# Attention scores over groups of 32 rows, two heads in one product, two units issued by turns

## The reference

```python
xs = x[:, global_idx, :]                      # 128 rows of each segment of 256
qh = xs.reshape(b, n_seg, k, NUM_HEADS, HEAD_DIM)
scores = jnp.einsum('bsqhd,bskhd->bshqk', qh, qh) * scale
attn = jax.nn.softmax(scores, axis=-1)
seg_out = jnp.einsum('bshqk,bskhd->bsqhd', attn, qh)
a_os = seg_out.reshape(b, n_seg * k, d)
a_denoms = a_os.sum(axis=-1)                  # the mixing weights come from these sums
```

## Time and profile before

| | |
|---|---|
| median of three runs | 1491.39 us (1488.74 to 1492.62) |
| the profiled execution | 1493.54 us |
| its span | 1491.6 us |
| TensorE busy in the span | 1366.6 us (92%) |
| VectorE busy | 885.0 us (59%) |
| GpSimd busy | 794.1 us (53%) |
| ScalarE busy | 656.6 us (44%) |
| granted TensorE clock, mean of the span | 0.959 |
| attention | from the start to about 139 us |

### The profile page before, as it was taken

How to read it: one execution, slowest core, us unless ns; L and a number is a source line. 1 busy time by engine, 2 the same in 40 slices (tenths; PEclk the granted TensorE clock), 3 DMA queues, 4 the chain that set the end, 5 groups by cost and what they waited for, 6 DMA issues and landing times. The chain is left out here.

```text
span 1491.6 us, 28870 instructions
## 1 busy us (share of the span) xinstructions
PE 1366.6 (92%) x9215; PEld 1202.3 (81%) x9216; DVE 885.0 (59%) x1767; ACT 656.6 (44%) x1170; POOL 794.1 (53%) x696
## 2 busy tenths in 40 slices
PE   8997599999999993899969999999999987999997
PEld 3444488888888883777768999999999977999997
DVE  5788422222222223577568887888888844666655
ACT  4554433233333331666544444543443434555553
POOL 6663197777660003231039887987887855350500
PEclk9997799999999997899979999999999998999999
DMA  4112425222220004210032274475465485465450
GB/s 166 56 33 74 136 79 155 95 98 99 101 96 11 13 15 134 68 57 1 1 113 85 80 205 126 143 195 132 148 187 143 145 286 191 155 214 184 149 201 30
DMA packets 112523, 171.45 MB, mean 115 GB/s; under 512 B 6384, under 2 KB 97648, under 8 KB 106320
## 3 DMA queue, kind: packets, MB, share of 16 engines
q1 hardware_dynamic: 103440, 156.27, 32.7%
q0 software_dynamic: 3408, 9.31, 2.2%
q10 hardware_dynamic: 5616, 5.11, 1.0%
HBM read 115.22 MB, written 55.44 MB: 114 GB/s over the span
## 5 line engine op out<-in xcount | busy, mean ns | idle before, releaser
L1992 PE MATMUL comb_psO<-hand_parts,comb_eh 128*128 (+1 forms) x1024 | 198.6, 292 | 0.9 <-DVE hand_parts L1485 0.6
L1731 ACT ACTIVATE disp_raw<-disp_psL 128x512 f32<-128x512 f32 x128 | 76.5, 598 | 198.7 <-PE disp_psL L1644 109.2
L1992 PEld LDWEIGHTS comb_psO<-hand_parts,comb_eh 128*128 128x128 f32 x1024 | 156.5, 190 | 1.7 <-DVE comb_el L2092 0.8
L1644 PE MATMUL disp_psL<-disp_ph,hand_xh 128*128 (+1 forms) x512 | 149.6, 292 | 5.7 <-DVE disp_e L1865 5.7
L1644 PE MATMUL disp_psL<-disp_ph,hand_xl 128*128 (+1 forms) x512 | 146.5, 286 | 0.0
L1644 PE MATMUL disp_psL<-disp_pl,hand_xh 128*128 (+1 forms) x512 | 146.5, 286 | 0.0
L1992 PE MATMUL comb_psO<-hand_parts,comb_el 128*128 (+1 forms) x512 | 143.8, 281 | 0.0
L2092 DVE TENSOR_TENSOR comb_el<-comb_psT,comb_eh 128x512 fp32r<-128x512 f32 x128 | 87.9, 688 | 85.6 <-ACT comb_eh L2026 82.9
L1667 PE MATMUL disp_psS<-disp_e,last_x 128*128 128x256 f32 x512 | 133.5, 384 | 5.1 <-POOL disp_e L1789 5.1
L1064 DVE TENSOR_TENSOR moe_hs<-moe_psH,moe_act_a 128x1024 f32<-128x1024 f32 x39 | 47.8, 1224 | 145.5 <-PE moe_psH L972 130.8
L972 PE MATMUL moe_psH<-w_hi,moe_xh 128*128 x312 | 127.9, 410 | 6.4 <-POOL w_lo L882 4.5
(11 more groups left out here) (273 smaller groups left out, 3931.1 us busy)
## 6 DMA issues: line engine op xcount, KB each, us to landing
logits<-disp_raw SPq DMA_DIRECT2D x64, 512.0 KB, 4.0
hand_e<-logits SPq DMA_DIRECT2D x32, 1024.0 KB, 6.5
w_raw<-in_w SPq DMA_DIRECT2D x8, 2048.0 KB, 7.8
disp_wt<-in_w_slot SPq DMA_DIRECT2D x16, 1024.0 KB, 9.8
w_raw<-in_w SPq DMA_DIRECT2D x8, 1024.0 KB, 10.5
disp_bt<-in_b_slot SPq DMA_DIRECT2D x16, 512.0 KB, 4.9
slot_y<-disp_slots SPq DMA_DIRECT2D x64, 128.0 KB, 3.2
comb_y_in<-slot_y SPq DMA_DIRECT2D x3, 2048.0 KB, 10.6
```

What stands on the lines that cost most here:

```text
L1644: last = nc.tensor.matmul(psL[p][:, b, :], xp[:, kd, t * P:(t + 1) * P], pp[:, half, kd, :].rearrange("p a n -> p (a n)"), start=b % 2 == ...
L1731: nc.scalar.activation(raw[mc % 4][:, half * 2:half * 2 + 2, :], psL[l_bank[mc]][:, half * 2:half * 2 + 2, :], ACT.Copy).then_inc(copied, 1)
L1992: last = nc.tensor.matmul(psO[j % 2][:, 0:D], ep[s % EB][:, i, :], yp[:, bass.ds(odd, 1), ch * D:(ch + 1) * D].rearrange("p a d -> p (a d) ...
```

## The change

The masked copies and the scores are made in another way. There is one masked copy of x for a segment, `xm[q]`, [128, 2 halves, 2 parities, 128], in which a group of 32 partitions (two heads) has its first or its second head left. It is made by one GpSimd product per segment, with a mask of two columns, `odd`, that VectorE sums up from the head mask at the start (one more of the `picked` steps). A unit's score is now two products, each of 32 rows and 256 columns: rows `(n * 2 + j) * 32` and on for unit n and row group j, two heads into half of the bank. Both units of a pair are issued in one call: j = 0 of unit 0, j = 0 of unit 1, a wait of TensorE for its own results (`rows_scored`), j = 1 of unit 0, j = 1 of unit 1. The wait for the exponents is one for both units, `p * 2 - 2`. `turn_max` stands behind both scores instead of between them.

```diff
-PICK_STEPS = 3
+PICK_STEPS = 4
+RG = 32
...
     dve.wait_ge(c["filled"], FIRST_STEPS)
+    v.tensor_reduce(c["odd"][:], c["headmask"][:].rearrange("p (r a) -> p a r", a=2), X, ALU.add).then_inc(c["picked"], 1)
...
-    dve.wait_ge(c["picked"], 2)
+    dve.wait_ge(c["picked"], 3)
...
-        xm = [m.sb(f"xm{i}", [P, UH, P]) for i in range(UPS)]
+        xm = [m.sb(f"xm{i}", [P, KD, 2, P]) for i in range(2)]
...
             def masks(i):
-                for k in range(2 * UPS):
-                    q, g = divmod(k, UPS)
-                    half, part = divmod(g, HG)
-                    if g == 0:
-                        wait(pool, xT_ready, i * 2 + (q + 1))
-                    wait(pool, scored, i * 8 + (k - UPS + 1))
-
+                for q in range(2):
+                    wait(pool, xT_ready, i * 2 + (q + 1))
+                    wait(pool, scored, i * 8 + (q - 1) * UPS)
                     nc.gpsimd.tensor_tensor(
-                        xm[g][:], xT[q][:, half, :].unsqueeze(1).to_broadcast([P, UH, P]),
-                        c["headmask"][:, part * UH:(part + 1) * UH].unsqueeze(2).to_broadcast([P, UH, P]),
-                        ALU.mult).then_inc(xm_ready, 1)
-                    if g == UPS - 1:
-                        seg = i * 2 + q - 2
-                        if not isinstance(i, int) or seg >= 0:
-                            weights.low_slice(pool, seg, w0_high)
+                        xm[q][:], xT[q][:].unsqueeze(2).to_broadcast([P, KD, 2, P]),
+                        c["odd"][:].unsqueeze(1).unsqueeze(3).to_broadcast([P, KD, 2, P]), ALU.mult).then_inc(xm_ready, 1)
+                    seg = i * 2 + q - 2
+                    if not isinstance(i, int) or seg >= 0:
+                        weights.low_slice(pool, seg, w0_high)
 
             fill_first(nc, c, pool)
             fill_constants(nc, c, pool)
+            pool.wait_ge(c["picked"], 1)
             masks(0)
...
-            def score(i, k, n):
+            def score(i, k):
                 at = pair(i, k, 0)
                 if at is None:
                     return
                 p, half = at
-                u, g, q = p * 2 + n, half * 2 + n, k // 2
-                wait(pe, xm_ready, u + 1)
-                wait(pe, prob_ready, u - (UPS - 1))
-                nc.tensor.matmul(psS[g][:].rearrange("p a b -> p (a b)"), xT[q][:, half, :],
-                                 xm[g][:].rearrange("p a b -> p (a b)"), start=True, stop=True).then_inc(scored, 1)
+                q = k // 2
+                wait(pe, xm_ready, i * 2 + (q + 1))
+                wait(pe, prob_ready, p * 2 - 2)
+                for j in range(UH // 2):
+                    if j == 1:
+                        wait(pe, rows_scored, p + 1)
+                    for n in range(2):
+                        rows = slice((n * 2 + j) * RG, (n * 2 + j + 1) * RG)
+                        last = nc.tensor.matmul(psS[half * 2 + n][:, 2 * j:2 * j + 2, :].rearrange("p a t -> p (a t)"),
+                                                xT[q][rows, half, :], xm[q][rows, half].rearrange("p a t -> p (a t)"),
+                                                start=j == 0, stop=True, skip_group_check=True)
+                        if j == UH // 2 - 1:
+                            last.then_inc(scored, 1)
+                        elif n == 1:
+                            last.then_inc(rows_scored, 1)
...
             def step(i, k):
-                score(i, k, 0)
+                score(i, k)
                 turn_max(i, k)
-                score(i, k, 1)
                 gather(i, k)
                 add_max(i, k)
```

More of the change, by code:

```diff
@@ L103, in constants @@
     c["headmask"] = m.sb("headmask", [P, HG * UH])
+    c["odd"] = m.sb("odd", [P, 2])
     c["pick_each"] = m.sb("pick_each", [2 * PH, PH // 2, 2, 2])
@@ L200, in dilated_attention @@
         even_loaded = [m.sem(f"even_loaded{i}") for i in range(2)]
-        w0_high = m.sem("w0_high")
+        w0_high, rows_scored = m.sem("w0_high"), m.sem("rows_scored")
         block = ctx.enter_context(nc.Block())
```

## The result

The changed kernel takes 1559.2 us (median of 4 runs, 1558.8 to 1560.2), the kernel before 1490.1 us beside it (4 runs): a ratio of 1.046, 95% interval 1.0445 to 1.0481. It is 69 us slower; the prediction was 1517 us with a range of 1508 to 1548. The profiled execution has a span of 1557.8 us against 1491.6.

A forecast was written before the change was run, and what follows sets the result against it. It took a chain through TensorE, VectorE and ScalarE to bound odd attention steps, TensorE even ones. Steps growing from 3.85 to 4.70 us (1.66 + 3.04) added 26 us to 1491.4: 1517 us, range 1508 to 1548.

The forecast's parts named there:

- What bounds the kernel: Attention before: odd steps bound by a TensorE, VectorE and ScalarE chain of 3.64 us, even steps by TensorE; 3.85 us average.
- both kinds have the same: Attention after: odd steps and even ones (with transposes of x and outputs) share one chain bound, 4.70 us.
- The score's own time: Two dependent score phases in attention: first unit scored 1.66 us after the start, between 1.45 and 1.88.
- my lower bound: First unit scored at 1.45 us if the other unit's product lies wholly beside the first.
- The chain: Attention step: 1.66 us of scoring plus 3.04 to the next start, 4.70 us against 3.85; +26 us in total.
- The clock: Rival in attention: idle TensorE loses the high clock; partly low 1526 to 1538 us (0.29), nearly throughout about 1559 (0.10).
- Clock mostly as before: Main case: longer attention chain with the clock mostly unchanged, 1517 us (1510 to 1525), chance 0.55.
- low nearly throughout: Rival: low clock in nearly all attention steps, 6.1 us each, about 1559 us, chance 0.10.
- the sign that I had named for this case: Granted clock leaving 1.00 between 20 and 130 us would show the prediction wrong.
- GpSimd's saving: Masked copies: four products per segment become one, 3.1 us less GpSimd work per segment, worth 0.
- It doesn't do what it says: Rival: the two units' row groups don't run beside each other; step 4.92 us, 1524 us, within the first case's range.
- The faster rival: TensorE's throughput bounds attention, so less score streaming gives steps below 3.85 us: 1466 to 1476 us, chance 0.03.

The follow-up runs named there:

- e1: Changed kernel with 30 extra products of the identity, once, between the first transpose of x and the first score: 1564.8 us, ratio 1.049.
- e3: Kernel before with only the change's order and its one wait for both exponents, scores still 128 rows by 512 columns: 1521.1 us, ratio 1.0213.
- e2: Changed kernel with extra products of the identity ending each TensorE step, five in odd and two in even steps: 1570.9 us, ratio 1.0508.
- e4: Kernel before with each score over the first 32 rows only, the heads in other rows left out: 1600.2 us, ratio 1.0737.
- e7: Kernel before with each unit's score over the 64 rows that hold its four heads: 1597.8 us, ratio 1.0732.
- f2: Changed kernel reordered: spread before maxima, exponents before next maxima's copy, shift before gather, transposed maxima before score: 1529.3 us, ratio 1.0253.
- f1: Kernel before reordered: spread before maxima, exponents before the copy of the next maxima, shift products before gather: 1490.5 us, ratio 0.9995.
- e6: Changed kernel without alternating units: both row groups of one unit, then the other unit: 1602.1 us, ratio 1.0757.
- f3: Kernel before with 64-row scores, both units' halves side by side behind one wait, in the order of f2: 1518.8 us, ratio 1.0179.
- f4_high_between: f1 with the ScalarE copy of the next maxima between the two exponents instead of behind both: 1489.5 us, ratio 0.9993.

## Why the prediction was wrong

*What bounds the kernel.* Right for the high clock: the odd step is a chain, and a score that needs less of TensorE brought nothing (4.47 us a step in e1 with 1.47 us of scoring, 4.47 in the first steps of e3 with 1.96). In the kernel as it ran, the start of a score was released by the second exponent only behind an odd step (5.74 us); the even ones took 6.40 us, and TensorE's own work at the low clock was their bound, where I had written that both kinds have the same.

*The score's own time.* I took 1.66 us for the first unit, between 1.45 and 1.88; at the high clock both are scored at 1.47. The row groups run wholly side by side, so my lower bound, 1.45, was the better value. The Trainium skill ("TensorE: Matmul & The Clock Gate", "Measured speedup vs the span model") gives a pack of tiles the time of one product and about 4 ns for each further tile, and these rows agree.

*The chain.* Predicted 4.70 us a step at the high clock, bounds 4.49 to 4.92. Measured 4.47 at e1's first start, 4.56 over seven steps of e2. So this part is worth (4.47 to 4.56 - 3.85) x 30 = +19 to +21 us where I had +26; only the score's 0.2 us was mis-sized. The changed order of full scores alone is 4.47 at the start of the stage and 4.6 on average: at one clock the row groups change a step by 0.1 us at most.

*The clock.* This is the step that failed. "Clock mostly as before" had 0.55, "low nearly throughout" 0.10, and the range left it out. Its price came out, 6.1 us a step and 1559 us against 6.04 us and 1559.2, but partly by luck: I had 3.1 us until both units are scored and 3.04 behind it in every step; measured were 2.52 and 3.22 in the odd steps, and the even ones are as long as TensorE's own work, 6.40. Its chance was wrong, because I asked only how long TensorE would be idle, against a stretch with 0.87 us of idle time that had kept the clock. I never asked how much of the array the new score would use. e4 and e7 show that this alone, with less idle time than before, keeps the clock low: 7.31 us a step. Of the 66 us, 19 to 21 are order and waits, (6.04 - 4.47 to 4.56) x 30 = 44 to 47 us the clock. The split depends on which is taken first: at the low clock the better order of f2 gave back 30 us. And the sign that I had named for this case, a granted clock that leaves 1.00 between 20 and 130 us, could not show it, because the column stood at 1.00.

*What would have pointed there.* The earlier trace rows had it half: the fall at the end of attention came when the score, in every step the largest of the full-size products, had just run out, and what was left was gather (four groups of 32 columns), shift (16 rows) and a narrow transpose. I read the 1.00 us of idle time and not the shapes. Both stand there together, so these rows alone would not have settled it.

*GpSimd's saving* of 3.1 us per segment I had put at nothing; no run takes it alone. In this order nothing waits for the masked copies, but f1 shows that it can be worth something in another. *"It doesn't do what it says"* fell: e6 shows the overlap. *The faster rival* fell too: with fewer rows the only steps below 3.8 us were three of f3 (3.38, 3.60 and 3.38 us), and two steps in a row took 7.6 us and more, where the kernel before takes 7.7.

What stays open: what the chip looks at precisely. The runs tell the height of the products from columns streamed, from idle time and from the streamed values, but not whether it counts rows in use at one moment, cells with weights, their sum over time or something that goes with them; weights of few columns were not tried alone. And e2 held either clock with the same steps, so whether scores of 64 rows would lose a high clock once they had it is not known.

## What to carry to other kernels

Products on a part of TensorE's rows save its time only while the rest of the rows is in use at the same moment, and in this kernel they cost the high clock: then all of its work in the stage takes up to twice as long, also the lines that the change doesn't touch. Before such a change, look at how much of a step's work still fills the array, and read the shapes of the products around the places where the clock fell. And judge the clock of a stage by the duration of an unchanged line, such as the gather's 0.64 or 1.08 us, not by the clock column alone.

## What the runs showed of the hardware that I had not expected

- 64 of 128 rows kept the clock at 1.2 GHz as surely as 32 did (steps of 7.31 us in both), with TensorE busy for 98% of the time and the same values other than zero streaming through. Two halves side by side got 2.4 GHz back in part.
- The clock column can stand at 1.00 over a stage at half clock, as it seems until the first change that the trace holds: 0.968 for the span of a kernel that was at half clock for its first 200 us, 0.900 for e1, whose low stretch is as long and whose trace holds the fall.
- The small VectorE instruction that makes the second half of the negated maxima (8 columns) takes 158 ns in the kernel after and 278 in the median, up to 783, before. These are its rows, of before and of after:

```profile
L462 DVE SCALAR_TENSOR_TENSOR att_negmax<-att_mx,att_negmax x26: 157/278/783, 20.5 to 116.9; 128x8 fp32r<-128x8 f32 x26
...
L469 DVE SCALAR_TENSOR_TENSOR att_negmax<-att_mx,att_negmax x28: 156/158/168, 24.6 to 188.6; 128x8 fp32r<-128x8 f32 x28
```

It waits for GpSimd. Each of the 13 that run under a masked copy before takes 0.39 us or more, and each of the 13 others 0.16 or 0.17; after, none of the 16 up to 120 us lies under one. The masked copies beside the odd step of the earlier trace rows, and two of these instructions:

```profile
71.12 0.16 DVE L462 SCALAR_TENSOR_TENSOR att_negmax<-att_mx,att_negmax 128x8 fp32r<-128x8 f32 x1
...
72.09 4.03 POOL L262 TENSOR_TENSOR att_xm<-att_xT,const_headmask 128x512 f32<-128x512 f32 x4 [1.66 <-ACT att_xT L406]
...
74.70 0.45 DVE L462 SCALAR_TENSOR_TENSOR att_negmax<-att_mx,att_negmax 128x8 fp32r<-128x8 f32 x1
```

The third of these copies starts at 74.09 and takes 1.04 us, so it ends at 75.13; the instruction ends at 75.15. In e3_order and f4_high_between too the long ones end 0.01 to 0.03 us behind the end of a masked copy.
